# Local attention in units of two: masks, scores, transposes and value products side by side, rotary sum on VectorE

## The chip, the cores and the metric

The kernel runs on one core of a Trainium2 chip. Its time is the device time of one execution of the whole program, in microseconds (us). Engines are named as the profile names them: PE (TensorE matmul), PEld (TensorE weight load), DVE (VectorE), ACT (ScalarE), POOL (GpSimd), SP (SyncE). SBUF is the memory the engines work in, PSUM the eight banks that PE writes.

## The reference

Four transformer layers on x of 16 x 512 x 128, each with an attention and a feed-forward part. The change lies in the feed-forward part of layer 1, which is itself a small transformer of two layers. Its attention, cut to what matters (8 heads of 64, windows of 64):

```python
h = shift_token(x)                          # second half of the features one token later
q, k, v = split(h @ wqkv)                   # 3 x 512
q, k = l2norm(q) * qs, l2norm(k) * ksc      # per head
q = q * cos * scale + rotate_half(q) * sin * scale
k = k * cos / scale + rotate_half(k) * sin / scale
sim = einsum('bhwid,bhwjd->bhwij', q * 8, look_around(k))    # own window and the one before
sim = where((i < j) | (i > j + WINDOW) | (j == -1), -max, sim)
x = x + einsum('bhwij,bhwjd->bhwid', softmax(sim), look_around(v)) @ wo
```

## The kernel before

The program is a row of phases; `local_attention_phase` runs twice, for the two small layers, from about 1860 to 2620 us and from about 2930 to 3694 us of the span. A batch (16 of them) has NT = 4 tiles of 128 tokens. A tile has PAIRS = 4 pairs of heads, and one pair of heads on one tile is a unit: UN = 16 units per batch. Each engine runs the same loop `steps`: iteration i, and in it steps s = 0 to 15, one unit each. There is no scheduler: the order on an engine is the order in which `step` calls its functions, and `Signal.wait(engine, batch, k)` waits for a semaphore to reach batch x (count per batch) + k. `trailing` names the unit that lies so many steps back.

Iteration i does the attention of batch i and, beside it, the projections of batch i + 1. For each tile of batch i + 1:
- PE `front` (L2461, L2462): q and k into the two halves of PJ, two banks of PSUM; ACT `square` reads them;
- DVE `straight` (L2660) and `crossed` (L2664, L2665): the products with the cosine and sine tables, from PJ into qk and rot;
- POOL `join` (L2614): qk + rot; DVE `lengths` (L2670) and `clip` (L2674): the sums of squares; POOL `scale`: their power -0.5 (L2618) and the product with qk (L2622);
- PE `values` (L2467): v into the second half of PJ, after `square` and `crossed` have read PJ; ACT `values_out` (L2559);
- PE `turn` (L2513): eight transposes of qk into both halves of PJ; DVE `queries_out` (L2693), ACT `keys_out` (L2579).

For each unit of batch i:
- PE `scores`: two masks (L2478, identity times a bf16 band) and two products (L2481) into PA; DVE `maximum` (L2679); ACT `exp` (L2566, two, with sums); DVE `invert` (L2683); POOL `normalise` (L2609);
- PE `turn_probs` (L2490), four transposes into PT (two in the first tile of a batch, whose keys are one block; its masks and scores have 128 columns instead of 192); ACT `probs_out` (L2573); PE `context` (L2501), four value products on two column halves of the array into PO.

For each tile of batch i: DVE `context_out` (L2688), PE `project_out` (L2521) into the first half of PJ, and DVE `add` (L2698), which adds PJ to H and counts h_added. PJ is one buffer, used in turn by front, values, turn and project_out.

Of the kernel before, what the change touches and what calls it, by code (L numbers as in the profile page):

```python
# [10 lines left out]
ALU = mybir.AluOpType  # L11
# [3 lines left out]
P = 128  # L15
# [2324 lines left out]
def local_attention_phase(net, name, l):  # L2340

    nc, H, d = net.nc, net.H, net.d
    UN = NT * PAIRS
    with ExitStack() as ctx:
# [24 lines left out]
        neg = sb("neg", [P, 4, 2])  # L2369
        total = sb("total", [P, 4, 2])  # L2370
        inv = sb("inv", [P, 4, 2])
# [26 lines left out]
        maxed = sig("maxed", UN)  # L2398
# [51 lines left out]
        def _(pe):  # L2450
# [17 lines left out]

            def scores(b, par, u):
                t, hp = divmod(u, PAIRS)  # L2470
                exped.wait(pe, b, 2 * (u - 1))
                if hp == 0:
                    q_here.wait(pe, b, t + 1)
                    k_here.wait(pe, b, t + 1)
                k0 = max(0, t * P - WINDOW)
                c0 = k0 - (t - 1) * P
                for e in range(2):
                    nc.tensor.matmul(PA[:, u % 2, e, c0:2 * P], net.ident_b[:], band[:, c0 - WINDOW:], start=True, stop=False)  # L2478
                for e in range(2):
                    rows = slice(e * DH64, (e + 1) * DH64)  # L2480
                    nc.tensor.matmul(PA[:, u % 2, e, c0:2 * P], qT[rows, par, hp, t * P:(t + 1) * P], kT[rows, par, hp, k0:(t + 1) * P],  # L2481
                                     start=False, stop=True).then_inc(scored.sem, 1)

            def turn_probs(b, u):
# [3 lines left out]
                for e in range(2):  # L2488
                    for kt in range(0 if t else 1, 2):
                        tr = nc.tensor.transpose(PT[:, 2 * e + kt], prob[:, u % 4, e, kt * P:(kt + 1) * P], ident)  # L2490
                tr.then_inc(p_turned.sem, 1)

            def context(b, par, u):
# [4 lines left out]
                for kt in range(0 if t else 1, 2):  # L2498
                    for e in range(2):
                        h = 2 * hp + e  # L2500
                        mm = nc.tensor.matmul(PO[e * DH64:(e + 1) * DH64, hp], v[:, par, t - 1 + kt, h * DH64:(h + 1) * DH64],  # L2501
                                              pt[:, u % 2, e, kt], start=(kt == 0 or t == 0), stop=(kt == 1),
# [3 lines left out]
            def turn(b, t):  # L2506
# [3 lines left out]
                h_added.wait(pe, b, t - 4)  # L2510
# [5 lines left out]
            def project_out(b, t):  # L2516
                c_out.wait(pe, b, t + 1)
                turned.wait(pe, b, 3 * (min(t + 7, (B - b) * NT) if isinstance(b, int) else t + 7))
                q_here.wait(pe, b, min(t + 5, (B - b) * NT) if isinstance(b, int) else t + 5)
# [3 lines left out]

            def step(i, par):
                for s in range(UN):
                    if has(i):
                        scores(i, par, s)
                    b, p, u = trailing(i, par, s, TR)
                    if has(b):
                        turn_probs(b, u)  # L2530
                    b, p, u = trailing(i, par, s, CT)
                    if has(b):
                        context(b, p, u)
                    if s % NT == 0 and has(i + 1):
                        front(i + 1, 1 - par, s // NT)
                    if s % NT == V_PROJ and has(i + 1):
                        values(i + 1, 1 - par, s // NT)
                    if s % NT == TURN % NT:
                        b, t = (i + 1, (s - TURN) // NT) if s >= TURN else (i, NT - 1)
                        if has(b):  # L2540
                            turn(b, t)
                    if s % NT == ADD % NT:
                        b, t = (i, (s - ADD) // NT) if s >= ADD else (i - 1, (s - ADD) // NT + NT)
                        if has(b):
                            project_out(b, t)

# [3 lines left out]
        def _(act):  # L2550
# [10 lines left out]
            def exp(b, u):  # L2561
                c0 = WINDOW if u >= PAIRS else P
                maxed.wait(act, b, u + 1)
                p_turned.wait(act, b, u - 3)
                for e in range(2):
                    nc.scalar.activation(prob[:, u % 4, e, c0:], PA[:, u % 2, e, c0:2 * P], ACT.Exp, bias=neg[:, u % 4, e:e + 1],  # L2566
                                         accum_out=total[:, u % 4, e:e + 1]).then_inc(exped.sem, 1)

            def probs_out(b, u):
                k0 = 0 if u >= PAIRS else 1  # L2570
                p_turned.wait(act, b, u + 1)
                pv_done.wait(act, b, u - 1)
                nc.scalar.activation(pt[:, u % 2, :, k0:], PT[:].rearrange("p (e k) n -> p e k n", e=2)[:, :, k0:],  # L2573
# [6 lines left out]

            def step(i, par):
                for s in range(UN):
                    b, p, u = trailing(i, par, s, TR)
                    if has(b):
                        probs_out(b, u)
                    if has(i):
                        exp(i, s)
                    if s % NT == 0 and has(i + 1):
                        square(i + 1, s // NT)
                    if s % NT == V_PROJ and has(i + 1):  # L2590
                        values_out(i + 1, 1 - par, s // NT)
                    if s % NT == TURN % NT:
                        b, p, t = (i + 1, 1 - par, (s - TURN) // NT) if s >= TURN else (i, par, NT - 1)
                        if has(b):
                            keys_out(b, p, t)
# [4 lines left out]
        def _(pool):  # L2600
# [4 lines left out]
            def normalise(b, u):  # L2605
                inverted.wait(pool, b, u + 1)
                c0 = WINDOW if u >= PAIRS else P
                pr = prob[:, u % 4, :, c0:]
                nc.gpsimd.tensor_tensor(pr, pr, inv[:, u % 4].unsqueeze(2).broadcast_to([P, 2, 2 * P - c0]),  # L2609
                                        ALU.mult).then_inc(normed.sem, 1)  # L2610
# [13 lines left out]
            def step(i, par):  # L2624
                for s in range(UN):
                    b, p, u = trailing(i, par, s, 1)
                    if has(b):
                        normalise(b, u)
                    if s % NT == JOIN and has(i + 1):
                        join(i + 1, s // NT)  # L2630
                    if s % NT == SCALE % NT:
                        b, t = (i + 1, (s - SCALE) // NT) if s >= SCALE else (i, NT - 1)
                        if has(b):
                            scale(b, t)
# [3 lines left out]
        def _(dve):  # L2638
# [27 lines left out]

            def lengths(b, t):
# [8 lines left out]
            def maximum(b, u):  # L2676
                c0 = WINDOW if u >= PAIRS else P
                scored.wait(dve, b, 2 * u + 2)
                nc.vector.tensor_reduce(neg[:, u % 4], PA[:, u % 2, :, c0:2 * P], AX, ALU.max, negate=True).then_inc(maxed.sem, 1)  # L2679

            def invert(b, u):
                exped.wait(dve, b, 2 * u + 2)
                nc.vector.reciprocal(inv[:, u % 4], total[:, u % 4]).then_inc(inverted.sem, 1)  # L2683
# [16 lines left out]
            def step(i, par):  # L2700
                for s in range(UN):
                    if has(i):
                        maximum(i, s)
                    b, p, u = trailing(i, par, s, 1)
                    if has(b):
                        invert(b, u)
                    if s % NT == 1 and has(i + 1):
                        straight(i + 1, s // NT)
                        crossed(i + 1, s // NT)
                    if s % NT == SUM and has(i + 1):  # L2710
                        lengths(i + 1, s // NT)
# [342 lines left out]
```

## Time and profile before

| | |
|---|---|
| median of 3 runs | 5757.93 us (5757.81 to 5766.5) |
| the profiled execution | 5767.75 us, its span 5765.9 us |
| busy over the span | PE 88%, DVE 61%, ACT 56%, POOL 41% |
| busy from 2300 to 2400 us, in the first of the two runs of the phase | PE 97.86, DVE 62.55, ACT 62.64, POOL 83.25 us of 100, granted clock 1.00 |
| local attention, two layers | about 750 us each |

Busy shares over the span are a mean over unlike phases; the row from 2300 to 2400 us is the one for this phase. In a timeline a row gives start, busy time, engine, line, operation and operands, and how many records it joins. An f32 matmul leaves two records (two passes), so x4 on L2481 are two matmuls. Busy time of a matmul holds its way through the array, which the next one overlaps, so what a piece costs is read from start to start.

### The profile page before, as it was taken

The numbers are of one execution on the slowest core, as the hardware profiler recorded it, in microseconds if no ns is written. First come the engines' busy times: TensorE is split into PE (matmuls) and PEld (weight loads), VectorE is DVE, ScalarE is ACT, GpSimd is POOL, SyncE is SP. The second block draws the span as 40 slices with busy tenths as digits, with TensorE's granted clock in tenths as the row PEclk, the third lists the DMA queues.
The fourth block names the chain that finished last, engine by engine and source line by source line (L and its number), as shares of the span: only waits on it lengthen the run. The fifth ranks groups of instructions, "written<-read, shape, count | busy, mean of one in ns | idle before, by whom it ended". The sixth has DMA issues, their size and how long they took to land. (4 is left out here: it accounts for less than half of the span.)

```text
span 5765.9 us, 106274 instructions
## 1 busy us (share of the span) xinstructions
PE 5074.1 (88%) x38604; PEld 2637.6 (46%) x38604; DVE 3496.2 (61%) x5697; ACT 3201.5 (56%) x7249; POOL 2337.4 (41%) x1954
## 2 busy tenths in 40 slices
PE   6999879988885899998889999897746999978998
PEld 2444334334442566664356666544421222225895
DVE  5787532277773566664356666446747999945444
ACT  2666643446674566665256666533522888873463
POOL 3333100122211788884078888400153232200766
PEclk7999989979997899999989999999855999997999
DMA  3343211133331000000100000000222233312222
GB/s 106 109 115 112 64 38 51 39 100 108 110 96 30 7 7 7 7 5 23 56 6 7 7 7 5 5 2 1 90 76 71 82 93 100 90 40 67 65 73 81
DMA packets 302987, 311.30 MB, mean 54 GB/s; under 512 B 74255, under 2 KB 244638, under 8 KB 300962
## 3 DMA queue, kind: packets, MB, share of 16 engines
q1 hardware_dynamic: 291362, 284.20, 17.1%
q0 software_dynamic: 11136, 20.59, 1.3%
q8 instruction: 306, 5.01, 0.4%
q14 instruction: 183, 1.50, 0.1%
HBM read 172.15 MB, written 123.99 MB: 51 GB/s over the span
## 5 line engine op out<-in xcount | busy, mean ns | idle before, releaser
L806 ACT ACTIVATE a_prob<-a_PB 128x512 f32<-128x512 f32 x2304 | 1253.1, 597 | 455.0 <-PE a_PB L648 341.0
L696 PE MATMUL a_PO<-a_prob,a_V 128*32 128x256 f32 (+3 forms) x8192 | 715.8, 422 | 22.6 <-ACT a_cn L779 22.3
L960 DVE TENSOR_REDUCE a_blocks<-a_PA 128x8 f32<-128x1024 f32 x512 | 602.2, 1215 | 38.8 <-PE a_PA L648 36.4
L963 DVE TENSOR_REDUCE a_neg<-a_PA 128x2 f32<-128x1024 f32 x512 | 591.0, 1213 | 34.7 <-PE a_PA L661 34.5
L661 PE MATMUL a_PA<-a_KS,a_QS 48*128 48x512 bf16 (+3 forms) x3072 | 471.4, 346 | 108.0 <-DVE a_blocks L960 67.1
L2679 DVE TENSOR_REDUCE f1a_neg<-f1a_PA 128x2 f32<-128x384 f32 (+1 forms) x512 | 267.1, 522 | 489.1 <-PE f1a_PA L2481 488.6
L2609 POOL TENSOR_TENSOR f1a_prob<-f1a_prob,f1a_inv 128x384 f32<-128x384 f32 (+1 forms) x512 | 395.4, 775 | 283.2 <-DVE f1a_inv L2683 283.2
L678 PE MATMUL a_PB<-a_QS,a_KS 51*128 51x512 bf16 (+3 forms) x3072 | 448.4, 329 | 56.6 <-ACT a_prob L806 55.0
L2573 ACT ACTIVATE f1a_pt<-f1a_PT 128x512 f32<-128x512 f32 (+1 forms) x512 | 278.7, 544 | 348.5 <-PE f1a_PT L2490 344.8
L2566 ACT ACTIVATE f1a_prob<-f1a_PA,f1a_neg 128x192 f32<-128x192 f32 (+1 forms) x1024 | 406.2, 405 | 67.9 <-DVE f1a_neg L2679 67.9
L661 PEld LDWEIGHTS a_PA<-a_KS,a_QS 48*128 48x128 bf16 x3072 | 123.7, 94 | 631.8 <-DVE a_blocks L960 197.3
L2618 POOL TENSOR_TENSOR f1a_ss<-f1a_ss,f1a_power 128x16 f32<-128x16 f32 x128 | 372.8, 2912 | 0.9
L860 POOL TENSOR_TENSOR a_qk<-a_qk,a_t 128x512 f32<-128x512 f32 x64 | 81.3, 1270 | 688.9 <-DVE a_t L930 688.9
L2614 POOL TENSOR_TENSOR f1a_qk<-f1a_qk,f1a_rot 128x1024 f32<-128x1024 f32 x128 | 301.2, 2353 | 65.7 <-DVE f1a_rot L2665 65.7
L2490 PE MATMUL f1a_PT<-ident,f1a_prob 128*128 128x128 f32 x1792 | 308.2, 289 | 1.9 <-POOL f1a_prob L2609 1.1
L2501 PE MATMUL f1a_PO<-f1a_pt,f1a_v 128*64 128x128 f32 x3584 | 308.8, 287 | 0.1
L2481 PE MATMUL f1a_PA<-f1a_kT,f1a_qT 64*128 64x192 f32 (+1 forms) x2048 | 293.3, 363 | 0.0
L696 PEld LDWEIGHTS a_PO<-a_prob,a_V 128*32 128x32 f32 x8192 | 163.3, 108 | 227.2 <-issue 127.4
L2622 POOL TENSOR_TENSOR f1a_qk<-f1a_qk,f1a_ss 128x1024 f32<-128x1024 f32 x128 | 243.8, 1904 | 10.0
L1181 ACT ACTIVATE f_hid<-f_ph,f_bias 128x512 f32<-128x512 f32 x192 | 132.0, 688 | 207.1 <-PE f_ph L1150 206.8
L2554 ACT ACTIVATE f1a_sq<-f1a_PJ 128x1024 f32<-128x1024 f32 x128 | 131.2, 1025 | 203.1 <-PE f1a_PJ L2462 203.1
L2490 PEld LDWEIGHTS f1a_PT<-ident,f1a_prob 128*128 128x128 f32 x1792 | 186.8, 141 | 104.7 <-issue 85.8
(450 smaller groups left out, 10236.0 us busy)
## 6 DMA issues: line engine op xcount, KB each, us to landing
a_spill<-a_qkp SPq DMA_DIRECT2D x96, 384.0 KB, 3.1
a_QS<-a_spill SPq DMA_DIRECT2D x384, 96.0 KB, 2.5
a_KS<-a_spill SPq DMA_DIRECT2D x384, 96.0 KB, 2.5
a_spill<-a_qkp SPq DMA_DIRECT2D x96, 256.0 KB, 3.1
a_raw<-a_cn SPq DMA_DIRECT2D x192, 72.0 KB
a_spill<-a_qkp SPq DMA_DIRECT2D x96, 128.0 KB, 3.0
tokens_out<-f_y SPq DMA_DIRECT2D x78, 128.0 KB
a_heads<-a_raw SPq DMA_DIRECT2D x32, 256.0 KB, 3.3
```

The costliest lines, as they stand in the source:

```text
L661: done.append(nc.tensor.matmul(PA[:, bank + e, c:c + w], QS[rows, par, pr, t * P:(t + 1) * P], KS[rows, par, pr, 0:w], start=(n == 0), sto ...
L678: done.append(nc.tensor.matmul(PB[:, bank[e], c:c + S - q0], KS[rows, par, pr, t * P:(t + 1) * P], QS[rows, par, pr, q0:S], start=(n == 0) ...
L696: mm = nc.tensor.matmul(PO[32 * j:32 * j + 32, first:last], V[:, par, t, 8 * e + pr], prob[:, k % st.ring, e, c + first - q0:c + last - q0 ...
L806: nc.scalar.activation(prob[:, k % st.ring, e], PB[:, ring_b.slot(0, ("b", s, e))], ACT.Exp, scale=scale).then_inc(pb_used, 1)
L960: nc.vector.tensor_reduce(to, of, AX, ALU.max).then_inc(pa_used, 1)
L963: nc.vector.tensor_reduce(neg[:, t, pr], PA[:, bank:bank + 2], AX, ALU.max, negate=True).then_inc(pa_used, 1)
L2490: tr = nc.tensor.transpose(PT[:, 2 * e + kt], prob[:, u % 4, e, kt * P:(kt + 1) * P], ident)
L2501: mm = nc.tensor.matmul(PO[e * DH64:(e + 1) * DH64, hp], v[:, par, t - 1 + kt, h * DH64:(h + 1) * DH64], pt[:, u % 2, e, kt], start=(kt == ...
L2566: nc.scalar.activation(prob[:, u % 4, e, c0:], PA[:, u % 2, e, c0:2 * P], ACT.Exp, bias=neg[:, u % 4, e:e + 1], accum_out=total[:, u % 4, ...
L2609: nc.gpsimd.tensor_tensor(pr, pr, inv[:, u % 4].unsqueeze(2).broadcast_to([P, 2, 2 * P - c0]), ALU.mult).then_inc(normed.sem, 1)
L2614: nc.gpsimd.tensor_tensor(qk[:, t], qk[:, t], rot[:], ALU.add).then_inc(joined.sem, 1)
L2618: nc.gpsimd.tensor_tensor(ss[:, t], ss[:, t], power[:], ALU.pow).then_inc(rooted.sem, 1)
```

## The change

It works on two units per step (s = 0, 2, 4, ...). A step with s divisible by 4 has `front` (and `turn` at its head), the other has `values` and `project_out`. On PE the order in a step is: `turn` | masks of both units | transposes of the unit five back | scores of both units | transposes of the unit four back and `front` (or `values`, `project_out`, transposes) | value products of the units six and five back. A mask matmul now covers two units at once (384 columns), the scores of two units share a bank, and one `maximum` reads 768 elements. prob, neg, total and inv get 8 places in place of 4, pt 4 in place of 2. `join` moves from POOL to DVE.

```diff
+    RING = 8
-        prob = sb("prob", [P, 4, 2, 2 * P])
-        pt = sb("pt", [P, 2, 2, 2, P])
+        prob = sb("prob", [P, RING, 2, 2 * P])
+        pt = sb("pt", [P, 4, 2, 2, P])
-        PA = psum("PA", [P, 2, 2, S])
+        PA = psum("PA", [P, 2, 2, 2, 2 * P])
-        TR, CT = 3, 4
-        JOIN, V_PROJ, SUM, CLIP, SCALE, TURN = 2, 2, 2, 3, 4, 7
-        OUT, ADD = 7, 10
+        LAG = 5
+        FRONT, V_PROJ, SCALE, TURN = 0, 2, 4, 8
+        OUT, ADD = 10, 14
+        def placed(i, par, s, lag):
+            if s % NT != lag % NT:
+                return (-1, 0, 0)
+            back = -((s - lag) // UN)
+            return (i - back, par if back % 2 == 0 else 1 - par, (s - lag + back * UN) // NT)
...
+            def masks(b, u):
+                exped.wait(pe, b, 2 * (u - 2))
+                c0 = WINDOW if u >= PAIRS else P
+                for e in range(2):
+                    nc.tensor.matmul(PA[:, (u // 2) % 2, e, :, c0:], net.ident_b[:],
+                                     band[:, c0 - WINDOW:].unsqueeze(1).broadcast_to([P, 2, 2 * P - c0]), start=True, stop=False)
             def scores(b, par, u):
-                exped.wait(pe, b, 2 * (u - 1))
-                    nc.tensor.matmul(PA[:, u % 2, e, c0:2 * P], net.ident_b[:], band[:, c0 - WINDOW:], start=True, stop=False)
+                    nc.tensor.matmul(scored_in(u)[:, e, c0:], qT[rows, par, hp, t * P:(t + 1) * P], kT[rows, par, hp, k0:(t + 1) * P],
+                                     start=False, stop=(u % 2 == 1)).then_inc(scored.sem, 1)
...
             def turn(b, t):
-                h_added.wait(pe, b, t - 4)
+                h_added.wait(pe, b, t - 5)
             def project_out(b, t):
+                h_added.wait(pe, b, t)
-            def join(b, t):
-                turned.wait(pool, b, 3 * t + 3)
-                nc.gpsimd.tensor_tensor(qk[:, t], qk[:, t], rot[:], ALU.add).then_inc(joined.sem, 1)
+            def join(b, t):
+                turned.wait(dve, b, 3 * t + 3)
+                nc.vector.tensor_tensor(qk[:, t], qk[:, t], rot[:], ALU.add).then_inc(joined.sem, 1)
             def maximum(b, u):
-                scored.wait(dve, b, 2 * u + 2)
-                nc.vector.tensor_reduce(neg[:, u % 4], PA[:, u % 2, :, c0:2 * P], AX, ALU.max, negate=True).then_inc(maxed.sem, 1)
+                scored.wait(dve, b, 2 * u + 4)
+                nc.vector.tensor_reduce(neg[:, u % RING:u % RING + 2], PA[:, (u // 2) % 2, :, :, c0:].rearrange("p e m n -> p m e n"), AX, ALU.max, negate=True).then_inc(maxed.sem, 1)
...
```

In the order a line counts instructions, not the two records of a timeline. The order on PE in one tile in the middle of a batch, before (two units and values behind a front; the rest of the tile repeats them, with turn):

```order
L2461 MATMUL f1a_PJ<-f1a_w,f1a_hs 128x512
L2462 MATMUL f1a_PJ<-f1a_w,f1a_hs 128x512
L2478 MATMUL f1a_PA<-f1a_band,ident_b 128x192 x2
L2481 MATMUL f1a_PA<-f1a_kT,f1a_qT 128x192 x2
L2490 MATMUL f1a_PT<-ident,f1a_prob 128x128 x4
L2501 MATMUL f1a_PO<-f1a_pt,f1a_v 64x128 x4
L2478 MATMUL f1a_PA<-f1a_band,ident_b 128x192 x2
L2481 MATMUL f1a_PA<-f1a_kT,f1a_qT 128x192 x2
L2490 MATMUL f1a_PT<-ident,f1a_prob 128x128 x4
L2501 MATMUL f1a_PO<-f1a_pt,f1a_v 64x128 x4
L2467 MATMUL f1a_PJ<-f1a_w,f1a_hs 128x512
L2521 MATMUL f1a_PJ<-f1a_c,f1a_wo 128x128 x4
```

and of the change, from the transposes ahead of the front to turn (L2506 transposes, L2473 and L2474 front, L2517 value products, L2485 masks, L2497 scores, L2479 values, L2538 project_out, L2529 turn):

```order
L2506 MATMUL f1a_PT<-ident,f1a_prob 128x128 x4
L2473 MATMUL f1a_PJ<-f1a_w,f1a_hs 128x512
L2474 MATMUL f1a_PJ<-f1a_w,f1a_hs 128x512
L2517 MATMUL f1a_PO<-f1a_pt,f1a_v 64x128 x8
L2485 MATMUL f1a_PA<-f1a_band,ident_b 128x2x192 x2
L2506 MATMUL f1a_PT<-ident,f1a_prob 128x128 x4
L2497 MATMUL f1a_PA<-f1a_kT,f1a_qT 128x192 x4
L2479 MATMUL f1a_PJ<-f1a_w,f1a_hs 128x512
L2538 MATMUL f1a_PJ<-f1a_c,f1a_wo 128x128 x4
L2506 MATMUL f1a_PT<-ident,f1a_prob 128x128 x4
L2517 MATMUL f1a_PO<-f1a_pt,f1a_v 64x128 x8
L2529 MATMUL f1a_PJ<-ident,f1a_qk 128x128 x8
```

Value products, masks, transposes and scores now stand once each between front and values, in groups of twice the size, where each stood twice; project_out is followed by one group of transposes and one of value products, and then by turn.

The order on DVE over one tile, before, from the products behind a front to context_out (queries_out follows):

```order
L2660 TENSOR_TENSOR f1a_qk<-f1a_PJ,f1a_tab 128x1024
L2664 TENSOR_TENSOR f1a_rot<-f1a_PJ,f1a_tab 128x16x32
L2665 TENSOR_TENSOR f1a_rot<-f1a_PJ,f1a_tab 128x16x32
L2679 TENSOR_REDUCE f1a_neg<-f1a_PA 128x2
L2683 RECIPROCAL f1a_inv<-f1a_total 128x2
L2670 TENSOR_REDUCE f1a_ss<-f1a_sq 128x16
L2698 TENSOR_TENSOR H<-f1a_PJ,H 128x128
L2679 TENSOR_REDUCE f1a_neg<-f1a_PA 128x2
L2683 RECIPROCAL f1a_inv<-f1a_total 128x2
L2674 TENSOR_SCALAR f1a_ss<-f1a_ss 128x16
L2688 COPY f1a_c<-f1a_PO 128x4x128
```

and of the change (L2695, L2699, L2700 the products; L2727 context_out, L2718 maximum, L2722 invert, L2704 join, L2709 lengths, L2713 clip, L2737 add, L2732 queries_out):

```order
L2695 TENSOR_TENSOR f1a_qk<-f1a_PJ,f1a_tab 128x1024
L2699 TENSOR_TENSOR f1a_rot<-f1a_PJ,f1a_tab 128x16x32
L2700 TENSOR_TENSOR f1a_rot<-f1a_PJ,f1a_tab 128x16x32
L2727 COPY f1a_c<-f1a_PO 128x4x128
L2718 TENSOR_REDUCE f1a_neg<-f1a_PA 128x4
L2722 RECIPROCAL f1a_inv<-f1a_total 128x2 x2
L2704 TENSOR_TENSOR f1a_qk<-f1a_qk,f1a_rot 128x1024
L2709 TENSOR_REDUCE f1a_ss<-f1a_sq 128x16
L2713 TENSOR_SCALAR f1a_ss<-f1a_ss 128x16
L2737 TENSOR_TENSOR H<-f1a_PJ,H 128x128
L2732 COPY f1a_qT<-f1a_PJ 128x4x128
```

Join has come in, context_out now stands ahead of the maximum, clip ahead of add, and add last before queries_out. On POOL four normalises and scale are left per tile.

## Rows read from the trace of the kernel before

**Rows 1.** Timeline, PE, 2309.5 to 2359: start, busy, engine, line, operation.
```profile
2309.59 1.13 PE L2461 MATMUL f1a_PJ<-f1a_w,f1a_hs 128*128 128x512 f32 x2
...
2323.70 0.33 PE L2478 MATMUL f1a_PA<-f1a_band,ident_b 128*128 128x192 bf16 x2
2323.96 0.60 PE L2481 MATMUL f1a_PA<-f1a_kT,f1a_qT 64*128 64x192 f32 x4
2324.49 0.66 PE L2490 MATMUL f1a_PT<-ident,f1a_prob 128*128 128x128 f32 x4
2325.08 0.66 PE L2501 MATMUL f1a_PO<-f1a_pt,f1a_v 128*64 128x128 f32 x8
2325.67 0.34 PE L2478 MATMUL f1a_PA<-f1a_band,ident_b 128*128 128x192 bf16 x2
...
2327.72 1.10 PE L2467 MATMUL f1a_PJ<-f1a_w,f1a_hs 128*128 128x512 f32 x2
2328.66 1.05 PE L2521 MATMUL f1a_PJ<-f1a_c,f1a_wo 128*128 128x128 f32 x8
2329.55 0.33 PE L2478 MATMUL f1a_PA<-f1a_band,ident_b 128*128 128x192 bf16 x2
...
2331.51 1.09 PE L2513 MATMUL f1a_PJ<-ident,f1a_qk 128*128 128x128 f32 x8
2332.44 0.33 PE L2478 MATMUL f1a_PA<-f1a_band,ident_b 128*128 128x192 bf16 x2
...
2334.39 1.13 PE L2461 MATMUL f1a_PJ<-f1a_w,f1a_hs 128*128 128x512 f32 x2
...
2336.22 0.33 PE L2478 MATMUL f1a_PA<-f1a_band,ident_b 128*128 128x192 bf16 x2
...
2358.25 1.12 PE L2461 MATMUL f1a_PJ<-f1a_w,f1a_hs 128*128 128x512 f32 x2
```
**Rows 2.** Timeline, ACT, 2323.5 to 2326; in brackets idle and its releaser.
```profile
2323.91 1.02 ACT L2554 ACTIVATE f1a_sq<-f1a_PJ 128x1024 f32<-128x1024 f32 x1 [1.10 <-PE f1a_PJ L2462]
```
**Rows 3.** Timeline, DVE, 2323.5 to 2338.
```profile
2325.18 1.20 DVE L2660 TENSOR_TENSOR f1a_qk<-f1a_PJ,f1a_tab 128x1024 f32<-128x1024 f32 x1
...
2327.50 0.55 DVE L2679 TENSOR_REDUCE f1a_neg<-f1a_PA 128x2 f32<-128x384 f32 x1
2327.96 0.15 DVE L2683 RECIPROCAL f1a_inv<-f1a_total 128x2 f32<-128x2 f32 x1
2328.03 1.20 DVE L2670 TENSOR_REDUCE f1a_ss<-f1a_sq 128x16 f32<-128x1024 f32 x1
2329.75 0.29 DVE L2698 TENSOR_TENSOR H<-f1a_PJ,H 128x128 f32<-128x128 f32 x1 [0.52 <-PE f1a_PJ L2521]
...
2331.02 0.34 DVE L2674 TENSOR_SCALAR f1a_ss<-f1a_ss 128x16 f32<-128x16 f32 x1
2331.62 0.69 DVE L2688 COPY f1a_c<-f1a_PO 128x512 f32<-128x512 f32 x1 [0.27 <-PE f1a_PO L2501]
2332.23 0.68 DVE L2693 COPY f1a_qT<-f1a_PJ 128x512 f32<-128x512 f32 x1
```
**Rows 4.** Timeline, POOL, 2328.5 to 2340.
```profile
2328.98 2.35 POOL L2614 TENSOR_TENSOR f1a_qk<-f1a_qk,f1a_rot 128x1024 f32<-128x1024 f32 x1
...
2334.07 0.83 POOL L2609 TENSOR_TENSOR f1a_prob<-f1a_prob,f1a_inv 128x384 f32<-128x384 f32 x1 [1.96 <-DVE f1a_inv L2683]
2334.86 2.91 POOL L2618 TENSOR_TENSOR f1a_ss<-f1a_ss,f1a_power 128x16 f32<-128x16 f32 x1
2337.84 1.91 POOL L2622 TENSOR_TENSOR f1a_qk<-f1a_qk,f1a_ss 128x1024 f32<-128x1024 f32 x1
```
**Rows 5.** Timeline, DVE in the slot experts' phase, 4203.5 to 4207.
```profile
4204.38 0.69 DVE L1671 TENSOR_TENSOR f_M<-f_kf,f_idxf 128x512 bf16<-128x512 f32 x1
```
**Rows 6.** Timeline, POOL in the same phase, 4203.5 to 4210.
```profile
4204.54 1.00 POOL L1620 TENSOR_TENSOR f_who<-f_seat,f_code 128x256 bf16<-128x256 bf16 x1 [0.71 <-DVE f_seat L1693]
...
4207.78 0.61 POOL L1620 TENSOR_TENSOR f_who<-f_seat,f_code 128x256 bf16<-128x256 bf16 x1 [0.71 <-DVE f_seat L1693]
```

More of the change, by code:

```diff
@@ L2517, in project_out @@
                 c_out.wait(pe, b, t + 1)
-                turned.wait(pe, b, 3 * (min(t + 7, (B - b) * NT) if isinstance(b, int) else t + 7))
-                q_here.wait(pe, b, min(t + 5, (B - b) * NT) if isinstance(b, int) else t + 5)
+                h_added.wait(pe, b, t)
+                turned.wait(pe, b, 3 * min(t + 8, (B - b) * NT))
+                q_here.wait(pe, b, min(t + 6, (B - b) * NT))
                 for j in range(PAIRS):
@@ L2522, in project_out, with probs_of, context_of @@
                 mm.then_inc(y_done.sem, 1)
-            def step(i, par):
-                for s in range(UN):
+            def probs_of(i, par, s, lag):
+                b, p, u = trailing(i, par, s, lag)
+                if has(b):
+                    turn_probs(b, u)
+            def context_of(i, par, s, lag):
+                b, p, u = trailing(i, par, s, lag)
+                if has(b):
+                    context(b, p, u)
+            def step(i, par):
+                for s in range(0, UN, 2):
+                    b, p, t = placed(i + 1, 1 - par, s, TURN)
+                    if s % NT == TURN % NT and has(b):
+                        turn(b, t)
+                    if has(i):
+                        masks(i, s)
+                    probs_of(i, par, s, LAG)
                     if has(i):
                         scores(i, par, s)
[L2528 to L2543, printed above, removed]
+                        scores(i, par, s + 1)
+                    if s % NT == FRONT:
+                        probs_of(i, par, s, LAG - 1)
+                        if has(i + 1):
+                            front(i + 1, 1 - par, s // NT)
+                    else:
+                        if has(i + 1):
+                            values(i + 1, 1 - par, s // NT)
+                        b, p, t = placed(i, par, s, ADD)
                         if has(b):
                             project_out(b, t)
+                        probs_of(i, par, s, LAG - 1)
+                    context_of(i, par, s, LAG + 1)
+                    context_of(i, par, s, LAG)
             steps(pe, step)
@@ L2624, in step @@
             def step(i, par):
[L2625 to L2632, printed above, removed]
+                for s in range(0, UN, 2):
+                    for lag in (2, 1):
+                        b, p, u = trailing(i, par, s, lag)
                         if has(b):
-                            scale(b, t)
+                            normalise(b, u)
+                    b, p, t = placed(i + 1, 1 - par, s, SCALE)
+                    if s % NT == SCALE % NT and has(b):
+                        scale(b, t)
             steps(pool, step)
```

114 lines of the change are left out of this document (62 added, 52 removed).

## The prediction

> **What bounds the kernel now.** The change touches one phase that runs twice (two layers, 16 batches each). I read the timeline of each engine over one batch in the middle of the first layer, TensorE (PE) first. The reader is to see that PE never idles there by more than a moment: from the first mask behind one front (2323.70) to the same point one tile later (2336.22) are 12.52 us [rows 1], and its pieces add up to 12.47: four units at 1.97 (2323.70 to 2325.67), the front 1.83 (2334.39 to 2336.22), values 0.94 (2327.72 to 2328.66), project_out 0.89, turn 0.93 (2331.51 to 2332.44). So PE is the bound, and the same sum of pieces, written for the new order, must be my tool. A batch of four tiles takes 48.66 (2309.59 to 2358.25), which is 1.42 less than 4 x 12.52, since the four units of a batch's first tile are narrower.
>
> **What the change takes from PE.** A pass of 128 f32 columns costs 0.11 (eight in project_out's 0.89). Four transposes at 0.11 make 0.44, and the group takes 0.59 [rows 1]: 0.15 is fixed. The eight passes of the value products run two at a time on two column halves, again 0.44 of 0.59. Scores: four passes of 192 in pairs, 0.33 of 0.53, fixed 0.20. Masks: bf16, some 0.16 of 0.26, fixed 0.10. A unit thus carries 0.60 of fixed time, and it comes where the form of the array changes (128x128, 64x128, 128x64). The order shows four changes of form for two units in place of eight. I split the fixed parts into about 0.10 for leaving a form and 0.05 to 0.11 for the first weights in the new one; two units then pay 0.57 instead of 1.20, and the front, now behind transposes, loses its 0.11. Columns stay the same, also those of the two masks of 384. Per tile: 5.48 columns + 2 x 0.57 + front 1.72 + values 0.94 + project_out 0.89 + turn 0.93 = 11.10, against 12.47. If PE stayed the bound, that would be -1.4 per tile, -150 us in all. Two waits don't let it.
>
> **First wait, values.** Values overwrites PJ, which square, straight and crossed must have read. Measured from F, the moment the front is issued: square starts at +0.21 and takes 1.02 [rows 2]; straight can start between +1.23 (its end) and +1.48 (where it stands now, behind a maximum) [rows 2, 3]; I take +1.33, as nothing stands between in the new order. The three rotary products take 2.32 (2325.18 to 2327.50) [rows 3], and PE follows 0.22 later: +3.88. Today PE has two units (3.94) to fill this, and starts values at +4.02. In the new order it has two value products (1.13), masks 0.32, transposes 0.54, scores 0.87 = 2.86, so it idles 1.0 per tile. That alone makes the tile 12.1.
>
> **Second wait, turn.** Turn writes PJ too, so it waits for the add of the project_out just before it (h_added, t - 5: by the step arithmetic that is always the add of the step directly ahead). PE gets there at 3.88 + 0.94 + 0.89 + 0.44 + 1.13 = +7.3. But DVE has the add at the end of its longest run. From the products' end at +3.65: context_out 0.61 (2331.62 to 2332.23), the maximum over 768, two reciprocals, join, lengths, clip, add. The maximum is not in the trace: 384 take 0.55 and a reduce of 1024 takes 1.20 [rows 3], on the line between them 0.94, of which 0.87 pass before the next can start; ends 0.55 and 1.20, and the middle is close since only the count differs. Reciprocals 0.07 each. Join is new on DVE: 1024 f32 as in straight or lengths, 1.20, some 1.15 to the next; bounds 1.12 and the 2.35 it took on POOL [rows 4], and I take DVE's own rows. Lengths 1.20. That puts clip at +7.6.
>
> Clip meets POOL. Today clip starts at 2331.02 and ends at 2331.36, and POOL's join ends at 2331.33 (2328.98 + 2.35) [rows 3, 4]: clip waits for POOL's running instruction. And POOL waits for a DVE instruction with two SBUF operands: the expert stage's L1620 takes 1.00 where L1671 started 0.16 ahead of it, and 0.61 where it did not [rows 5, 6]. Join is such an instruction and two normalises are released just behind it. So they start at join's end, +6.5, take 0.79 and 0.83 [rows 4] to +8.1, and clip, arriving within them, is done at +8.13. Add 0.29 [rows 3], signal 0.14: turn starts at +8.6, 1.3 after PE stood ready. From there PE has no cover left up to the next F: turn 0.93, masks 0.32, transposes 0.54, scores 0.87, transposes 0.49, front 1.72 = 4.87. Tile: 8.61 + 4.87 = 13.5, against 12.52 today. Without any meeting on the port: clip done at +7.7, turn at +8.1, tile 13.0.
>
> The Trainium skill (SBUF — State Buffer, section Who interferes with whom) states that a VectorE instruction with two SBUF inputs and a GpSimd one that reads SBUF block each other, whichever starts second waiting in full. My rows show one direction of it only. By the rule join would also wait for the tail of POOL's scale, and this speaks against moving join: POOL's mult would end near +5.5 (pow 2.91 and mult 1.91 behind two normalises [rows 4]), join is ready at +5.3, so everything shifts by 0.25, tile 13.7, 5889 us.
>
> **What else moves.** The deeper rings (8 for prob and its sums, 4 for pt) and LAG 5 mean that exp, normalise and the copies are needed a step later; ACT has the same instructions in a longer tile, so I cost them at nothing; the nearest is square, with an exp directly ahead of it, and each 0.1 that this exp is late makes the tile 0.1 longer. POOL loses 2.35 per tile, which nobody waits for now. The memset over a doubled prob lies beside the loads. Prologue: front to turn is the same chain as before. Tail: one more lag but less per step, 0 within 3 us per layer.
>
> **The sum.** The narrow units of a batch's first tile now save 1.2 (only those between turn and front count, and one maximum; bounds 1.0 and 1.4). Batch: 4 x 13.48 - 1.2 = 52.7, +4.06. This holds for batches 1 to 14 of each layer, 28 in all: +114. In batch 0 no add is awaited: 4 x 12.12 - 1.4 = 47.1, -1.6, twice: -3. Batch 15 has no front and no values, so PE's saving shows: 0.3 per unit on 16 units less a little for its turns, -4, twice: -8. Together +103. The profiled execution took 5767.75 (span 5765.9), 9.8 above the median of 5757.93; 5871 in its terms, **5861** against the median.
>
> **Rivals.** (a) The add is in time, and the tile ends at the first wait. It decides at turn: if DVE's run from the products to the add takes 3.4 or less rather than 4.8, PE arrives last. Then 12.12 per tile, batch 47.1, -1.56 x 28 - 11 = -55: 5703, faster. For it: PE's own saving is certain, and a reader who counts busy shares sees DVE far from full. Against: eight instructions stand in that run in order, each with a row. Chance 0.12; with a run between the two (tile 12.5, nothing changes) another 0.05.
> (b) POOL takes the port first each time: join starts only after both normalises, at +7.2, turn at +10.1, tile 15.0, batch 58.6, +9.95 x 28 - 11 = +268: 6026. Against: clip got in right at the end of POOL's join. 0.06.
> (c) The change doesn't save what it says: the second unit's scores use the same row halves and pay the fixed 0.20 again. In the step with the front nothing covers it: +0.2 per tile, 5885. The skill (TensorE: Matmul & The Clock Gate, section The mechanism) has weights load beside a running matmul only where the row group differs, which would give this; the second passes of a unit's own scores fit into 0.53, which speaks against. 0.07.
> (d) The forecast, port meetings more or fewer (5807 to 5889): 0.70.
>
> **Chances and range.** 0.2% is 12 us, what a measurement of this kernel can tell from none. Slower: (b), (c), (d) = 0.83; same 0.05; faster 0.12. The forecast's cases span 5807 to 5889; with (c) and errors of 0.2 per tile (22 us) I take 5790 to 5930, leaving out (a), (b) and a little.
>
> **What would show it.** Two idles of PE per tile: near 1.0 ahead of values, ended by the rotary products, and 0.8 to 1.5 ahead of turn, ended by the add (L2737). Front to front 13.0 to 13.7 in batches 1 to 14, near 12.1 in batch 0. Join near 1.2; normalises in the join's step stretched beyond 0.83; clip beyond 0.15. A group of two units' scores in 0.87, not 1.07. I am wrong if turn is released by anything but the add, or the tile is under 12.5.

## The result, and the profile after

| | before | after |
|---|---|---|
| median | 5760.83 us (5757.81 to 5766.5, 4 runs) | 5842.51 us (5836.66 to 5845.19, 4 runs) |
| ratio | 1 | 1.014, 95% interval 1.0124 to 1.0156 |
| profiled execution | 5767.75, span 5765.9 | 5836.66, span 5834.9 |
| a batch, front to front | 48.66 | 51.60 |
| PE busy, 2300 to 2400 us | 97.86 | 82.59 |

The change makes the kernel slower by 1.4%. The forecast was 5861, also slower. The first part of the page of after:

```profile
span 5834.9 us, 105096 instructions
## 1 busy us (share of the span) xinstructions
PE 4896.3 (84%) x38080; PEld 2609.5 (45%) x38092; DVE 3604.0 (62%) x5569; ACT 3182.9 (55%) x7249; POOL 2157.7 (37%) x1826
```

PE is busy for less time than before (84% for 88%) and the program is longer: PE has less work and waits more. Where it waits, the timeline of PE shows over one tile in the middle of the first layer. It is the longest tile of its batch, the one with no narrow units in it ("the full tile" below): front to front, the four tiles of a batch take 12.40, 12.87, 13.23 and 13.09. A row gives start, busy time, engine, line and operation, and in brackets the idle time ahead and what ended it. The rows answer to [rows 1]:

```profile
2353.34 1.02 PE L2474 MATMUL f1a_PJ<-f1a_w,f1a_hs 128*128 128x512 f32 x2
2354.30 1.09 PE L2517 MATMUL f1a_PO<-f1a_pt,f1a_v 128*64 128x128 f32 x16
2355.32 0.50 PE L2485 MATMUL f1a_PA<-f1a_band,ident_b 128*128 128x384 bf16 x2
2355.66 0.60 PE L2506 MATMUL f1a_PT<-ident,f1a_prob 128*128 128x128 f32 x4
2356.19 0.92 PE L2497 MATMUL f1a_PA<-f1a_kT,f1a_qT 64*128 64x192 f32 x8
2358.02 1.10 PE L2479 MATMUL f1a_PJ<-f1a_w,f1a_hs 128*128 128x512 f32 x2 [0.92 <-DVE f1a_rot L2700]
2358.96 1.05 PE L2538 MATMUL f1a_PJ<-f1a_c,f1a_wo 128*128 128x128 f32 x8
2359.85 0.60 PE L2506 MATMUL f1a_PT<-ident,f1a_prob 128*128 128x128 f32 x4
2360.38 1.09 PE L2517 MATMUL f1a_PO<-f1a_pt,f1a_v 128*64 128x128 f32 x16
2362.61 1.06 PE L2529 MATMUL f1a_PJ<-ident,f1a_qk 128*128 128x128 f32 x8 [1.14 <-DVE H L2737]
```

The two waits of the forecast stand there: values for the last rotary product, turn for the add. Over the four tiles of a batch the first is 0.92 to 1.35 and the second 0.54 to 1.62. Between them PE's pieces have become cheaper: from start to start the value products of two units take 1.02 for twice 0.59 [rows 1].

DVE in the same tile, answering to [rows 3]:

```profile
2355.46 1.23 DVE L2695 TENSOR_TENSOR f1a_qk<-f1a_PJ,f1a_tab 128x1024 f32<-128x1024 f32 x1 [2.23 <-ACT f1a_sq L2583]
...
2357.80 0.68 DVE L2727 COPY f1a_c<-f1a_PO 128x512 f32<-128x512 f32 x1
2358.39 0.94 DVE L2718 TENSOR_REDUCE f1a_neg<-f1a_PA 128x4 f32<-128x768 f32 x1
2359.26 0.21 DVE L2722 RECIPROCAL f1a_inv<-f1a_total 128x2 f32<-128x2 f32 x2
2359.39 1.38 DVE L2704 TENSOR_TENSOR f1a_qk<-f1a_qk,f1a_rot 128x1024 f32<-128x1024 f32 x1
2360.70 1.21 DVE L2709 TENSOR_REDUCE f1a_ss<-f1a_sq 128x16 f32<-128x1024 f32 x1
2361.94 0.34 DVE L2713 TENSOR_SCALAR f1a_ss<-f1a_ss 128x16 f32<-128x16 f32 x1
2362.19 0.28 DVE L2737 TENSOR_TENSOR H<-f1a_PJ,H 128x128 f32<-128x128 f32 x1
```

and POOL, answering to [rows 4]:

```profile
2357.79 1.90 POOL L2659 TENSOR_TENSOR f1a_qk<-f1a_qk,f1a_ss 128x1024 f32<-128x1024 f32 x1
2359.65 2.59 POOL L2650 TENSOR_TENSOR f1a_prob<-f1a_prob,f1a_inv 128x384 f32<-128x384 f32 x2
```

From 2355.46 to 2362.47 DVE has no gap of note, and the add that the turn needs is the last of that run, though project_out had given it its data by 2360.01 (2358.96 + 1.05). The join takes 1.38 where lengths of the same size takes 1.21: it starts 0.3 ahead of the end of POOL's mult (2357.79 + 1.90). The two normalises behind it take 2.59 where a pair elsewhere takes 1.61: the first stands until the join is through. Clip then ends with them, at 2362.28. By the rule of the Trainium skill (SBUF — State Buffer, section Who interferes with whom) a VectorE instruction with two SBUF inputs and a GpSimd one that reads SBUF block each other. The rows of the join agree, and in both directions: 0.18 longer behind the mult, and two normalises 0.98 longer behind it; [rows 5, 6] had shown one direction.

### The profile page after: what moved, and what is told of

It is laid out like the page before. It is cut to its first block and busy times, and to the rows that moved or that the text cites. A ratio compares the mean times of both kernels' runs of the same rounds, so it can differ in the third digit from the quotient of the medians.

```text
span 5834.9 us, 105096 instructions
## 1 busy us (share of the span) xinstructions
PE 4896.3 (84%) x38080; PEld 2609.5 (45%) x38092; DVE 3604.0 (62%) x5569; ACT 3182.9 (55%) x7249; POOL 2157.7 (37%) x1826
## 5 line engine op out<-in xcount | busy, mean ns | idle before, releaser
L2650 POOL TENSOR_TENSOR f1a_prob<-f1a_prob,f1a_inv 128x384 f32<-128x384 f32 (+1 forms) x512 | 502.2, 1001 | 523.3 <-DVE f1a_inv L2722 522.2
L2695 DVE TENSOR_TENSOR f1a_qk<-f1a_PJ,f1a_tab 128x1024 f32<-128x1024 f32 x128 | 156.8, 1225 | 325.7 <-ACT f1a_sq L2583 325.7
L2718 DVE TENSOR_REDUCE f1a_neg<-f1a_PA 128x4 f32<-128x768 f32 (+1 forms) x256 | 226.6, 885 | 175.5 <-PE f1a_PA L2497 175.5
L2479 PE MATMUL f1a_PJ<-f1a_w,f1a_hs 128*128 128x512 f32 x256 | 149.0, 665 | 173.8 <-DVE f1a_rot L2700 173.8
L2506 PE MATMUL f1a_PT<-ident,f1a_prob 128*128 128x128 f32 x1792 | 286.4, 277 | 5.8 <-ACT f1a_pt L2602 1.6
L2529 PE MATMUL f1a_PJ<-ident,f1a_qk 128*128 128x128 f32 x1024 | 143.8, 286 | 137.1 <-DVE H L2737 126.3
L2517 PE MATMUL f1a_PO<-f1a_pt,f1a_v 128*64 128x128 f32 x3584 | 253.1, 280 | 0.2
L2659 POOL TENSOR_TENSOR f1a_qk<-f1a_qk,f1a_ss 128x1024 f32<-128x1024 f32 x128 | 243.5, 1902 | 10.0
L2517 PEld LDWEIGHTS f1a_PO<-f1a_pt,f1a_v 128*64 128x64 f32 x3584 | 190.6, 136 | 112.3 <-issue 111.6
```

The lines of the kernel that those rows point to most:

```text
L2506: tr = nc.tensor.transpose(PT[:, 2 * e + kt], prob[:, u % RING, e, kt * P:(kt + 1) * P], ident)
L2650: nc.gpsimd.tensor_tensor(pr, pr, inv[:, u % RING].unsqueeze(2).broadcast_to([P, 2, 2 * P - c0]), ALU.mult).then_inc(normed.sem, 1)
```

## Where the 82 us come from

From the first front to the last add a layer's attention takes 819.5 and 821.9 before, 860.3 and 862.3 after: +81, which accounts for the 82 between the medians. (The two profiled executions differ by 69 only, since that of before spent 12 more outside these two stretches.) A batch in the middle is 2.94 longer (51.60 less 48.66), 28 of them +82. The batches at the two ends of a layer change by 1 us or less each.

Over the phase, the groups of PE's rows by line (busy time, mean ns, and idle ahead with its releasers); first before, then after:

```profile
L2467 PE MATMUL f1a_PJ<-f1a_w,f1a_hs 128*128 128x512 f32 x256 | 148.6, 663 | 66.2 <-DVE f1a_rot L2665 61.2
L2513 PE MATMUL f1a_PJ<-ident,f1a_qk 128*128 128x128 f32 x1024 | 146.5, 288 | 4.7 <-ACT f1a_v L2559 4.7
```
```profile
L2479 PE MATMUL f1a_PJ<-f1a_w,f1a_hs 128*128 128x512 f32 x256 | 149.0, 665 | 173.8 <-DVE f1a_rot L2700 173.8
L2529 PE MATMUL f1a_PJ<-ident,f1a_qk 128*128 128x128 f32 x1024 | 143.8, 286 | 137.1 <-DVE H L2737 126.3 <-ACT f1a_v L2588 7.4 <-POOL f1a_qk L2659 3.4
```

PE's two waits grow by 240 us (66.2 + 4.7 to 173.8 + 137.1). The time grows by 82, so PE's own work is some 158 shorter: the change does what it says, and the waits take it all and half as much again.

## The experiments

"Full tile" is the tile shown above; the turn's place in it is counted from the start of front's second product (2353.34), where it comes at +9.27 in after. Ratios are to the kernel before. The waits in the last column are sums over both layers, 128 tiles, in us.

| run | median us | ratio, 95% | batch | waits of values, of turn for the add |
|---|---|---|---|---|
| after | 5842.5 | 1.014 (1.0124 to 1.0156) | 51.60 | 173.8, 126.3 |
| add after join | 5716.7 | 0.9923 (0.9903 to 0.9943) | 47.17 | 173.8, none |
| join on POOL | 5750.6 | 0.9988 (0.9977 to 1.0) | 48.11 | 174.0, 27.8 |
| add before clip | 5806.1 | 1.0079 (1.0061 to 1.0097) | 50.30 | 174.0, 89.1 |
| before, join on DVE | 5761.3 | 0.9996 (0.9987 to 1.0006) | 48.67 | 61.2, none |
| forms apart | 5898.4 | 1.0241 (1.0224 to 1.0258) | 53.65 | 173.9, 118.5 |
| add, then forms | 5687.7 | 0.9877 (0.986 to 0.9893) | 46.16 | 97.5, 9.6 |
| halves alone | 5859.6 | 1.0174 (1.0157 to 1.0191) | 51.5 to 54.7 | 83.6, 199.6 |
| all of these | 5663.5 | 0.9824 (0.9808 to 0.984) | 45.73 | 31.4, 74.2 |
| halves, scale first | 5736.8 | 0.9956 (0.9938 to 0.9973) | 48.50 | 83.7, 115.9 |
| scale first | 5822.6 | 1.0103 (1.0086 to 1.012) | 51.24 | 173.9, 115.9 |
| all, scale first | 5589.4 | 0.9704 (0.9688 to 0.972) | 43.35 | 31.1, 9.6 |

**Add behind the join.** In DVE's step with the values:

```diff
                             join(i + 1, s // NT)
-                            lengths(i + 1, s // NT)
-                            clip(i + 1, s // NT)
                         b, p, t = placed(i, par, s, ADD)
                         if has(b):
                             add(b, t)
+                        if has(i + 1):
+                            lengths(i + 1, s // NT)
+                            clip(i + 1, s // NT)
```

> The changed kernel with one order on DVE altered: in the step with the values, the add of project_out comes right behind the join, ahead of lengths and clip. Theory (the turn waits for DVE's add, which stands last in DVE's run): the add is done lengths and clip earlier, near 6.7 us behind the front, before PE reaches the turn at 7.3; the wait of 1.1 ahead of the turn goes, the tile falls from 13.2 to 12.1, a batch to some 47.0, and 28 batches x 4.6 off 5842 give about 5713, faster than both kernels. Rival (what holds the turn is not DVE's order but the port or the chain from join to scale, which comes due next): the wait only changes its releaser, and the time stays within 10 of 5842.

Measured 5716.65: 126 less than after, by one change of order.

```profile
L2529 PE MATMUL f1a_PJ<-ident,f1a_qk 128*128 128x128 f32 x1024 | 146.9, 289 | 13.9 <-ACT f1a_v L2588 7.0 <-POOL f1a_qk L2659 3.4
```

The releaser "DVE H" is gone, the 126.3 with it, and nothing takes its place. The turn's wait is DVE's order.

**Join back on POOL**, behind the two normalises of its step:

```diff
+                    if s % NT == V_PROJ and has(i + 1):
+                        join(i + 1, s // NT)      # POOL
...
-                            join(i + 1, s // NT)      # DVE
```

> The changed kernel with the rotary sum (join) given back to POOL, behind its two normalises of the step with the values; the rest of the change stays. Theory (join on DVE is 1.4 us of the run ahead of the add): the run gets that much shorter, but clip may be held by POOL's normalises until 7.2 us behind the front; the turn starts at 7.6, tile 12.4, about 5750; with no meeting at the port the turn is in time and the time is that of the first wait alone, 5713. Rival 1 (the two-unit order itself is what costs): stays near 5842. Rival 2 (POOL becomes late with scale): the turn of the next steps waits for the scaled rows instead, above 5800.

Measured 5750.59, the value with the meeting at the port. That meeting is in the rows, DVE first, then POOL:

```profile
2324.95 1.20 DVE L2711 TENSOR_REDUCE f1a_ss<-f1a_sq 128x16 f32<-128x1024 f32 x1
2326.18 0.67 DVE L2715 TENSOR_SCALAR f1a_ss<-f1a_ss 128x16 f32<-128x16 f32 x1
```
```profile
2325.21 1.61 POOL L2650 TENSOR_TENSOR f1a_prob<-f1a_prob,f1a_inv 128x384 f32<-128x384 f32 x2
2326.78 2.36 POOL L2655 TENSOR_TENSOR f1a_qk<-f1a_qk,f1a_rot 128x1024 f32<-128x1024 f32 x1
```

Clip, 0.17 where nothing holds it, takes 0.67 and ends with the second normalise (2326.82). With the join gone from DVE the normalises take 1.61 again.

**Add ahead of clip**, on DVE:

```diff
                             lengths(i + 1, s // NT)
-                            clip(i + 1, s // NT)
                         b, p, t = placed(i, par, s, ADD)
                         if has(b):
                             add(b, t)
+                        if has(i + 1):
+                            clip(i + 1, s // NT)
```

> The changed kernel with add ahead of clip on DVE (join, lengths, add, clip). Theory that POOL's normalises hold the clip and with it the add: the add no longer stands behind the held clip, the turn starts 0.3 earlier in each tile, 12.9, 5842 - 0.3 x 4 x 28 = about 5810. Rival (the add itself is then held by the same two normalises, since they keep whichever DVE instruction comes next waiting): no change within 10 of 5842.

Measured 5806.12, 36 less than after; the turn comes at +8.90 for +9.27. The rival is out: the add, with one operand in PSUM and one in SBUF, starts within the same two normalises (on POOL from 2321.69, 2.57) and takes what it takes elsewhere:

```profile
2322.71 1.21 DVE L2709 TENSOR_REDUCE f1a_ss<-f1a_sq 128x16 f32<-128x1024 f32 x1
2323.84 0.28 DVE L2737 TENSOR_TENSOR H<-f1a_PJ,H 128x128 f32<-128x128 f32 x1
```

**The kernel before with join on DVE.**

```diff
                     if s % NT == SUM and has(i + 1):
+                        join(i + 1, s // NT)
                         lengths(i + 1, s // NT)
```

> The kernel before with one part of the change alone: join on DVE ahead of lengths, everything else as it was. Theory (the slower time comes from DVE's run ending after PE is ready, which the old order does not have): PE stays the bound and covers the join, within 15 of 5761. Rival (join costs by itself wherever it stands, by DVE's 1.2 us and by blocks with POOL): slower by 50 or more, with PE waiting ahead of turn or values.

Measured 5761.27, the same time. The join takes 1.21 there, the add behind it (2325.48) is done 0.9 or more ahead of the turn, and PE stays the bound. So neither half of the change is slow by itself: DVE's longer run costs nothing under the old order, and the new order with join on POOL is no slower than before.

**Forms of the array apart.** In the step with the front:

```diff
-                    probs_of(i, par, s, LAG)
                     if has(i):
                         scores(i, par, s)
+                    probs_of(i, par, s, LAG)
+                    if has(i):
                         scores(i, par, s + 1)
```

> The changed kernel with the two units' scores of the front's step kept apart again: masks, scores of s, transposes, scores of s + 1, transposes, front. The work is the same, two more changes of the array's form stand in the stretch between turn and front, which no wait covers. Theory (a change of form costs 0.15 to 0.18): 0.31 to 0.36 more per tile, at 112 tiles 35 to 40, near 5880, and up to 0.3 a tile more if the first transposes come before ScalarE has their probabilities. Rival (changes of form cost nothing, the fixed parts of the groups are something else): 5842, within 10.

Measured 5898.39, 56 more than after. Of these 26 are a wait (rows by line, this run):

```profile
L2506 PE MATMUL f1a_PT<-ident,f1a_prob 128*128 128x128 f32 x1792 | 290.8, 279 | 29.3 <-ACT f1a_pt L2609 27.9
```

for the transposes' bank, which ScalarE must have read (1.6 in after). The turn's wait is 8 shorter. 56 - 26 + 8 = 38 over 112 tiles is 0.34 for two changes of form: 0.17 each, within the 0.15 to 0.18 expected here and the 0.15 to 0.21 that the prediction had split off. Changes of form cost; the rival is out.

**Add behind join, and transposes into the first wait.** On DVE as in the first run, and on PE:

```diff
                     else:
+                        probs_of(i, par, s, LAG - 1)
                         if has(i + 1):
                             values(i + 1, 1 - par, s // NT)
                         b, p, t = placed(i, par, s, ADD)
                         if has(b):
                             project_out(b, t)
-                        probs_of(i, par, s, LAG - 1)
```

> The kernel with add right behind the join, and on PE the second transposes of the values' step moved ahead of values. Theory (with add in time the tile is bounded by the first wait, of values for the rotary products, and then only by work that PE has left over): 0.5 of work moves into the wait, the wait falls from about 0.9 to 0.4, and the turn still finds the add done or nearly: tile 11.6 to 11.9, 5660 to 5690. Rival (add is only just in time, so that the wait comes back ahead of the turn): 5717, as with the add alone.

Measured 5687.67, ratio 0.9877. The wait of values falls from 173.8 to 97.5, and the turn's for the add is 9.6.

**Halves.** Square and straight in two, one per half of PJ, so that ScalarE starts as soon as the first half is written:

```diff
-                nc.scalar.activation(sq[:].rearrange("p a h n -> p a (h n)"), PJ[:], ACT.Square).then_inc(squared.sem, 1)
+                for a in range(2):
+                    projected.wait(act, b, 2 * t + a + 1)
+                    nc.scalar.activation(sq[:, a].rearrange("p h n -> p (h n)"), PJ[:, a], ACT.Square).then_inc(squared.sem, 1)
...
-                nc.vector.tensor_tensor(qk[:, t], x, table(0, t), ALU.mult).then_inc(turned.sem, 1)
+                for a in range(2):
+                    squared.wait(dve, b, 2 * t + a + 1)
+                    nc.vector.tensor_tensor(qk[:, t, a], x[:, a], table(0, t)[:, a], ALU.mult).then_inc(turned.sem, 1)
```

> The changed kernel with square and straight each split into two halves, one per half of PJ (queries, keys): the first square may run while PE still writes the second half, and DVE's straight starts behind it. Everything behind it on DVE, down to the add, is as in the changed kernel. ScalarE is free 0.3 to 0.5 ahead of the whole square, the second straight stands behind the second square, and the split costs some 0.14 on DVE. Theory (a tile's length is the chain front, square, rotary products, DVE's run, add, turn, front): values and turn both come 0.6 to 0.8 earlier behind the front, 112 tiles x 0.7 = 78, about 5765. Rival (something beside this chain, as POOL's scale and its two normalises, sets when clip and add may go): values come earlier, the turn does not, and the time stays within 15 of 5842.

Measured 5859.64, where I had expected 5765. Values come 0.69 earlier, as expected. The turn stays at +9.27 in the full tile. DVE and then POOL of such a tile:

```profile
2298.09 2.07 DVE L2706 TENSOR_TENSOR f1a_qk<-f1a_qk,f1a_rot 128x1024 f32<-128x1024 f32 x1
2300.08 1.21 DVE L2711 TENSOR_REDUCE f1a_ss<-f1a_sq 128x16 f32<-128x1024 f32 x1
```
```profile
2294.20 2.90 POOL L2656 TENSOR_TENSOR f1a_ss<-f1a_ss,f1a_power 128x16 f32<-128x16 f32 x1
2297.18 1.90 POOL L2660 TENSOR_TENSOR f1a_qk<-f1a_qk,f1a_ss 128x1024 f32<-128x1024 f32 x1
2299.04 2.59 POOL L2651 TENSOR_TENSOR f1a_prob<-f1a_prob,f1a_inv 128x384 f32<-128x384 f32 x2
```

The join is ready 0.7 earlier and takes 0.87 more than its 1.20, until the mult is through at 2299.08. In the full tile of after the join met only the mult's last 0.18, by coincidence: DVE's chain and POOL's end at nearly the same moment there. My theory, that one chain sets the tile, was short of the second; the rival had the mechanism, values earlier and the turn not. (Why the run is even 17 us slower than after is told with the clock, in the last section.)

> The same split in the kernel with add behind the join and the second transposes ahead of values. There the waits for the rotary products are 97.5 in all. Theory: each tile gets the lesser of 0.7 and its wait, 128 tiles, some 70 to 85 less, so 5600 to 5620, and PE is then the bound with 11.1 per full tile. Rival (another engine comes due: ScalarE with square between two exp, or the add again): 5650 or more, with the wait of values gone and another in its place.

With the same split on top of the two good changes: 5663.5, not 5600 to 5620; the rival's case. The wait of values goes (97.5 to 31.4), and the turn waits for the add again (9.6 to 74.2); the join takes 1.91 in the mean.

**Scale ahead of the normalises.** Clip is done well before POOL starts on scale (2301.66 against 2307.43 in the halves run); scale stands behind two normalises that wait for the reciprocals. On POOL:

```diff
+                    b, p, t = placed(i + 1, 1 - par, s, SCALE)
+                    if s % NT == SCALE % NT and has(b):
+                        scale(b, t)
                     for lag in (2, 1):
                         b, p, u = trailing(i, par, s, lag)
                         if has(b):
                             normalise(b, u)
-                    b, p, t = placed(i + 1, 1 - par, s, SCALE)
-                    if s % NT == SCALE % NT and has(b):
-                        scale(b, t)
```

> The kernel with square and straight in halves (5860), and on POOL scale ahead of the two normalises of its step instead of behind them. There DVE's join took 1.89 in the mean (2.07 in the full tiles) against 1.21 for the lengths of the same size, and it ended with POOL's mult. Theory (the join stands still until the mult is through, and the mult is that late because pow and mult queue behind normalises that wait for the reciprocals, though clip is done 4 before): pow and mult run in POOL's idle stretch, the join takes 1.2, the turn comes at 8.0 instead of 8.84, 0.68 to 0.86 less per tile: 5745 to 5785. Rival (join is slow for another reason, or mult holds another instruction of DVE in its new place): 5840 or more, join still near 1.9, or another DVE instruction stretched by as much.

5736.83, 123 less than halves alone and somewhat below the range, since the falls of the clock, some 35 us of the halves run (last section), are gone too: the clock is 1.00 from 2000 to 2600 us. A batch takes 48.50, for 51.53 in the halves run where the clock did not fall. In the groups by line the join takes what lengths takes:

```profile
L2711 DVE TENSOR_REDUCE f1a_ss<-f1a_sq 128x16 f32<-128x1024 f32 x128 | 155.0, 1211 | 0.0
L2706 DVE TENSOR_TENSOR f1a_qk<-f1a_qk,f1a_rot 128x1024 f32<-128x1024 f32 x128 | 154.2, 1205 | 0.3
```

The same instruction took 1889 ns without that move, so its length was POOL's doing alone.

> The changed kernel with that move of scale alone. Theory: there the join is held only by the mult's last 0.18 (mean 1.29 against 1.21), so it gives back 0.08 to 0.17 per tile, 10 to 20: 5822 to 5835. Rival (POOL's late mult is what really sets the turn in the changed kernel too, through clip and the normalises behind it): 5780 or less.

5822.64, 20 less in the medians. In the traces the two layers' attention is 15 shorter: 0.36 in each of 28 batches (51.24 for 51.60) make 10, and 3.4 are waits of the turn for POOL's scale (L2659) that are gone; the rest of the 20 is within the spread of the runs. POOL's mult did not set the turn there, whose wait for the add only falls from 126.3 to 115.9; DVE's order did.

> The same move in the kernel with add behind join, transposes ahead of values, and halves (5663). Theory: join 1.91 to 1.2, so the add is there 0.7 earlier and the waits ahead of turn (74 in all) go but for a little: 5590 to 5610, PE the bound. Rival: the add is held by another engine, 5640 or more.

5589.4, ratio 0.9704 (0.9688 to 0.972), 3% faster than before and 4.3% faster than after. A batch takes 43.35, and PE has nothing of note to wait for:

```profile
L2529 PE MATMUL f1a_PJ<-ident,f1a_qk 128*128 128x128 f32 x1024 | 145.7, 288 | 18.6 <-DVE H L2739 9.6 <-ACT f1a_v L2589 9.0
L2479 PE MATMUL f1a_PJ<-f1a_w,f1a_hs 128*128 128x512 f32 x256 | 143.4, 643 | 34.0 <-DVE f1a_rot L2702 31.1
```

This is what the kernel gains once three engines are ordered for the two-unit order. How much of it the old order would gain by the same moves was not run; there PE waits 71 in all ahead of values and turn (66.2 + 4.7), so that shorter waits alone could not make up the 170 or so by which the last run is ahead of before.

## Why the prediction was right, step by step

- PE's saving. Right. The four changes of form per two units and the shorter groups are there (value products 1.02 start to start, scores 0.85 for two units). The forms-apart run puts a change at 0.17. The full tile of after less its two waits is 13.23 - 0.92 - 1.14 = 11.17, and with PE the bound the last run's tiles take 10.72 to 10.93 front to front; the prediction had 11.10 for the full tile.
- First wait, values. Right: 0.92 for 1.0 in the full tile, released by L2700 in all 128 tiles.
- Second wait, turn. Right in mechanism and releaser, and confirmed by undoing it alone (-126 us). Counted as in the prediction, from the moment that front is issued (2354.20: its second product starts at 2353.34 and takes 0.86, as the first does), the turn comes at +8.41 for +8.61. The maximum of 768 takes 0.94, as interpolated; clip ends at +8.08 for +8.13, and the add starts 0.09 ahead of clip's end, where I had it behind.
- The port. Right that clip is held to the end of the normalises and that they are held by the join. By the rule of the Trainium skill (SBUF — State Buffer, section Who interferes with whom) join would also wait for the tail of the scale, for which I had 0.25. It does: it waits 0.18. The forecast of 5861 left that out and 5889 held it; with the turn 0.2 early elsewhere neither figure shows it alone, but the scale-first run does: 0.36 per batch.
- Rival (c), the second unit's scores paying 0.20 again: refuted, two units' scores take 0.85, not 1.07. The units' scores use the two row halves in turn, so each follows one of the other half, and the condition that the prediction quotes for hidden weights is met also from one unit to the next: the rival did not follow from it. (Its price was also summed 2 too high: 0.2 x 4 x 28 on 5861 is 5883, not 5885.) Rivals (a) and (b) did not come true: the join gets the port first, and the add is not in time.
- The sum. Of the excess of forecast over result (103 against 82): the full tile 13.23 for 13.48, that is 1.0 per batch, and narrow units 1.32 for 1.2, together 1.12 x 28 = -31. On the other side +10 from the ends of a layer, where I had taken 3 and 8 off and the traces show 1. The two errors partly cancel, which is luck: with the ends right the forecast would have been 10 further off.
- Those ends are the one step that failed: "Batch 15 has no front and no values, so PE's saving shows". The saving is there, 7.60 per tile for 8.87 in steps without turn. But two things take most of it back. PE, with no front to do, runs into POOL's scale at the first turn of the batch:

```profile
2681.96 0.76 PE L2529 MATMUL f1a_PJ<-ident,f1a_qk 128*128 128x128 f32 x5 [1.68 <-POOL f1a_qk L2659]
```

  and the tail is longer by a lag: from the end of the last scores to the last project_out 12.2 (2701.64 to 2713.84) for 7.9 (2670.34 to 2678.27), not "0 within 3". Batch 0, forecast at -1.6, took +0.2 (48.21 for 48.04 in the first layer): values waits 7.3 in it, 2.79 in its first tile, for 3.4 before, and the turn 1.6 for ScalarE's values_out (L2588), where it had waited for nothing.

## What to carry to other kernels

When work is regrouped to save on the bounding engine, write out the order of every engine that it waits for, and place in each what that engine's next instruction releases: here one add, with its data there and last in its queue, took 126 us: with it in its place the kernel is 44 us faster than before, without it 82 slower. In this kernel a buffer shared by four users (PJ) turned the latest reader's queue into the tile's length. And before moving work between DVE and POOL, look for what the other runs at that time, also a few tenths away: here an edit that shifted DVE by 0.7 met POOL's mult for 0.87.

## What was not expected of the hardware

- The blocking between DVE and POOL goes both ways and ends with the running instruction: a join of 1.21 took 2.07 behind a mult (up to 2.29 in the halves run), a pair of normalises took 2.59 for 1.61 behind a join, a clip of 0.17 took 0.67. Lengths (1.20 to 1.22) and add (0.27 to 0.29, one operand in PSUM) were not held in any run. Clip and lengths both have one SBUF operand, and only clip is held; what sets them apart no run here shows.
- The clock. In the halves run the turn waits 1.33 to 2.11 per tile, for 0.54 to 1.62 in after, and behind some of these waits the granted clock falls. Its PE timeline, and the windows of 1 us around it (window, length, PE busy, granted clock, DMA share, GB/s):

```profile
2457.72 1.67 PE L2529 MATMUL f1a_PJ<-ident,f1a_qk 128*128 128x128 f32 x8 [1.83 <-DVE H L2739]
```
```profile
2456.00:2457.00 1.00, 0.00 (x0) 1.00 0.00 0
2457.00:2458.00 1.00, 0.28 (x3) 1.00 0.00 0
2458.00:2459.00 1.00, 1.00 (x8) 0.51 0.06 16
2459.00:2460.00 1.00, 1.00 (x5) 0.50 0.00 0
2460.00:2461.00 1.00, 1.00 (x7) 0.50 0.00 0
2461.00:2462.00 1.00, 1.00 (x9) 0.78 0.00 0
```

  The lower level, 1.2 GHz, is granted for some 3.5 us behind an idle time of 1.83, and the turn takes 1.67 for 1.06. Most waits of that length are followed by the full clock, as at 2302.00 or 2353.54; why these and not the others, no run shows. Over 2000 to 2200 us the clock is 0.97 in that run and 1.00 in after. Batches of the halves run without such a fall take 51.53, as those of after (51.60), and those with falls 0.9 to 3.2 more, together some 18 per layer. The first two batches of a layer, where PE waits for the rotary products and not for the add, together are 8.7 and 9.7 shorter than in after. The sum, +9.1 in the first layer and +8.3 in the second, is the 17 us by which the run came out above after.
